# A GRU tile on TensorE: the sums' products ahead of the wait for the turned state, one PSUM bank moved from the ring of the sums to the candidate's state part

## The reference, cut to what matters

```python
h = relu(layernorm(x))
x = x + conv3(relu(conv2(relu(conv1(h)))))        # conv(h) = segment_sum((h @ W)[src] * norm, dst) + b
h = relu(layernorm(x))
red = segment_sum(h[src] + relvectors[rel], dst)  # 3125 x 256
gi, gh = red @ w_ih.T + b_ih, h @ w_hh.T + b_hh   # 3125 x 768 each
r = sigmoid(gi_r + gh_r);  z = sigmoid(gi_z + gh_z)
n = tanh(gi_n + r * gh_n)
x = x + (1 - z) * n + z * h
```

## Time and profile before

| what | value |
|---|---|
| runs | 934.06, 934.55, 934.75 us, median 934.55 |
| the profiled execution's own time | 933.93 us |
| its span, first to last instruction | 930.0 us |
| TensorE (PE) busy | 886.0 us, 95% |
| VectorE (DVE) busy | 444.3 us, 48% |
| ScalarE (ACT) busy | 290.0 us, 31% |
| granted TensorE clock, mean over the span | 0.992 |

### The profile page before, as it was taken

One profiled execution on the slowest core, in us unless ns is written; L12 is line 12 of the kernel. 1 busy time (PEld: TensorE's weight loads), 2 busy tenths in 40 slices (PEclk: granted clock), 3 DMA queues, 4 the chain that ended last, 5 costly groups with the idle time before them and its releaser, 6 DMA issues.

```text
span 930.0 us, 16580 instructions
## 1 busy us (share of the span) xinstructions
PE 886.0 (95%) x5495; PEld 529.4 (57%) x5495; DVE 444.3 (48%) x1164; ACT 290.0 (31%) x609; POOL 75.5 (8%) x244
## 2 busy tenths in 40 slices
PE   2779999999999999999999999999999999999996
PEld 1348777777777865444444544445464455555553
DVE  7956888888887201021112413336253133334345
ACT  3365566666666311011111202222231111222122
POOL 0210111000000025551000000000000000000000
PEclk9989999999999999999999999999999999999999
DMA  6100000000000410000000101111401000000101
GB/s 191 30 2 2 4 22 17 16 16 22 17 16 16 144 32 3 3 3 1 1 0 24 44 14 39 46 46 51 137 20 31 10 25 24 23 23 23 30 28 31
DMA packets 37009, 28.50 MB, mean 31 GB/s; under 512 B 12870, under 2 KB 35554, under 8 KB 36925
## 3 DMA queue, kind: packets, MB, share of 16 engines
q1 hardware_dynamic: 36252, 26.97, 9.6%
q10 hardware_dynamic: 672, 0.41, 0.2%
HBM read 17.56 MB, written 9.81 MB: 29 GB/s over the span
## 4 chain that ended last, share of the span: by engine, by line
PE 92%; DVE 5%; issue 1%; ACT 1%; SPq 0%; DMA 0%; DVEq 0%
PE ps L1233 42%; PE ps L905 12%; PE ps L807 10%; PE ps L642 9%; PE ps L1244 5%; PE ps L646 5%; PE ps L1263 2%; PE ps L886 2%; DVE node_b L914 1%; PE ps L842 1%; PE ps L854 1%; PE ps L874 1%; PE ps L627 1%; PE ps L818 0%; DMA count<-in_dst 0%
## 5 line engine op out<-in xcount | busy, mean ns | idle before, releaser
L1233 PE MATMUL ps<-count,node_b 128*128 128x512 f16 (+3 forms) x1400 | 270.5, 351 | 0.4 <-DVE node_b L1395 0.3
L807 PE MATMUL ps<-node_b 128*128 128x175 f16 x808 | 192.9, 259 | 13.7 <-issue 7.8
L1233 PEld LDWEIGHTS ps<-count,node_b 128*128 128x128 f16 (+2 forms) x1400 | 121.5, 98 | 142.1 <-issue 7.3
L905 PE MATMUL ps<-node_a,count 128*128 128x256 f16 x1050 | 200.7, 277 | 0.2 <-DVE node_a L1026 0.2
L914 DVE TENSOR_TENSOR node_b<-node_b 128x1024 f16<-128x1024 f16 (+2 forms) x303 | 161.7, 587 | 0.0
L1109 ACT ACTIVATE count<-ps 128x500 f32 x202 | 122.8, 608 | 96.7 <-PE ps L807 94.9
L1233 PE MATMUL ps<-count,node_a 128*128 128x512 f16 (+2 forms) x700 | 134.7, 352 | 0.0
L807 PEld LDWEIGHTS ps<-node_b 128*128 128x128 f16 x808 | 79.8, 99 | 62.7 <-issue 28.4
L905 PEld LDWEIGHTS ps<-node_a,count 128*128 128x128 f16 x1050 | 101.1, 100 | 4.2 <-ACT count L1109 0.4
L1233 PEld LDWEIGHTS ps<-count,node_a 128*128 128x128 f16 (+1 forms) x700 | 60.0, 97 | 73.9 <-issue 7.1
L1325 DVE SCALAR_TENSOR_TENSOR work<-ps,dinv,params 128x256 f32<-128x256 f32 (+1 forms) x25 | 12.0, 480 | 125.0 <-PE ps L1244 125.0
(11 more groups left out here) (210 smaller groups left out, 787.9 us busy)
## 6 DMA issues: line engine op xcount, KB each, us to landing
node_a<-in_x SPq DMA_DIRECT2D x4, 768.0 KB, 8.4
table_scratch<-agg SPq DMA_DIRECT2D x21, 128.0 KB, 1.8
node_b<-table_scratch SPq DMA_DIRECT2D x3, 768.0 KB, 6.6
xt<-x_scratch SPq DMA_DIRECT2D x16, 128.0 KB, 2.1
out<-scaled SPq DMA_DIRECT2D x16, 128.0 KB, 1.7
xt<-in_x SPq DMA_DIRECT2D x12, 128.0 KB, 2.0
params<-in_x SPq DMA_DIRECT2D x12, 128.0 KB, 2.0
x_scratch<-xt SPq DMA_DIRECT2D x12, 128.0 KB, 1.7
```

The lines of the kernel that those rows point to most:

```text
L807: return PE.matmul(window(s)[:, :, keys], low, key_hot[k][:, j, :, i].rearrange("p (t w) -> p t w", w=SPAN), start=(s == 0 and j == 0), st ...
L905: last = PE.matmul(out_slot(u)[0:m, :], count[:, t, u * P:u * P + m], node_a[:, t, part, :], start=(t == 0 and part == 0), stop=(t == T - ...
L1233: last = PE.matmul(ps[:, b, 0:cols], nodes[0:k, t, part, f * P:(f + 1) * P], count[0:k, t, c * CHUNK:c * CHUNK + cols], start=(n == 0 and ...
```

## The change

`AGG_RING` becomes 2, so that the groups of sums use banks 0 and 1 and TensorE waits ahead of group h for the evacuation of group h - 2, in all three stages. Bank 2 takes the candidate's state part. On TensorE, a GRU tile's two r and z matmuls from the sums are issued ahead of the wait for `h_out`; then come the two from the state, the candidate's two from the state (bank 2, behind a new wait `nh_read` for VectorE's read of the tile before, signal `nh_done`), and last the candidate's two from the sums (`n_done`). On VectorE, the state part is read after `nh_done`, the bias of the input part is added ahead of the wait for `n_done`, and the sum with PSUM comes last and releases the tanh. The matmuls, activations, VectorE operations and DMAs are the same in number and size.

```diff
--- before.py
+++ after.py
@@ -30,7 +30,7 @@
 SETTLE_FIRST, SETTLE_ODD, SETTLE_STEP = 11, 8, 17
 OUT_SLOTS = 3
 BEATS = 4
-AGG_RING = 3
+AGG_RING = 2
 LOADS = 4
 
 
@@ -232,7 +232,7 @@
         x1_tile = [xt[0][:, :], xt[1][:, :], piece(flat_a, D, F32)]
         h_tile = [scaled[0][:, :], scaled[1][:, :], piece(flat_a, D, F32)]
         AHEAD = len(x1_tile)
-        H_BANK, RZ_BANK, N_BANK = 3, (4, 5), (6, 7)
+        NH_BANK, H_BANK, RZ_BANK, NI_BANK = 2, 3, (4, 5), (6, 7)
         assert at_piece[0] <= T * 2 * D
 
 
@@ -559,8 +559,8 @@
         x1_in = [sem(f"x1_in{k}") for k in range(AHEAD)]
         out_done = [sem(f"out_done{k}") for k in range(AHEAD)]
         gru_w_in, gru_b_in = sem("gru_w_in"), sem("gru_b_in")
-        h_made, h_turned, h_out, rz_done, n_done, biased, gates, n_sum, n_due, new_n, z_used, result = (sem(n) for n in (
-            "h_made", "h_turned", "h_out", "rz_done", "n_done", "biased", "gates", "n_sum", "n_due", "new_n", "z_used", "result"))
+        h_made, h_turned, h_out, rz_done, nh_done, nh_read, n_done, biased, gates, n_sum, new_n, z_used, result = (sem(n) for n in (
+            "h_made", "h_turned", "h_out", "rz_done", "nh_done", "nh_read", "n_done", "biased", "gates", "n_sum", "new_n", "z_used", "result"))
 
         def gru_load_sp(order, i):
             t = order[i]
@@ -615,7 +615,7 @@
                 gru_turn_act(order, i + 1)
             ACTE.wait_ge(biased, i + 1)
             ACTE.activation(gate_rz[k][0:m, :], gate_rz[k][0:m, :], ACT.Sigmoid).then_inc(gates, 1)
-            ACTE.wait_ge(n_due, i + 1)
+            ACTE.wait_ge(n_sum, i + 1)
             ACTE.activation(work[k][0:m, :], work[k][0:m, :], ACT.Tanh).then_inc(new_n, 1)
 
         def gru_turn_pe(order, i):
@@ -632,25 +632,30 @@
             if i == 0:
                 gru_turn_pe(order, 0)
                 PE.wait_ge(gru_w_in, 32)
-            PE.wait_ge(h_out, i + 1)
             if i >= 2:
                 PE.wait_ge(n_sum, i - 1)
-            rz, nn = RZ_BANK[k], N_BANK[k]
+            rz, ni = RZ_BANK[k], NI_BANK[k]
             hs = [h_t[k][:, f, 0:m] for f in range(HALVES)]
-            for n, (l, w, f) in enumerate([(sums[f], w_ih_sb, f) for f in range(HALVES)] +
-                                          [(hs[f], w_hh_sb, f) for f in range(HALVES)]):
-                done = PE.matmul(ps[0:m, rz, 0:2 * D], l, w[:, f, 0:2 * D], start=(n == 0), stop=(n == 2 * HALVES - 1))
+            for f in range(HALVES):
+                PE.matmul(ps[0:m, rz, 0:2 * D], sums[f], w_ih_sb[:, f, 0:2 * D], start=(f == 0), stop=False)
+            PE.wait_ge(h_out, i + 1)
+            for f in range(HALVES):
+                done = PE.matmul(ps[0:m, rz, 0:2 * D], hs[f], w_hh_sb[:, f, 0:2 * D], start=False, stop=(f == HALVES - 1))
             done.then_inc(rz_done, 1)
-            for col, ls, w in ((0, sums, w_ih_sb), (D, hs, w_hh_sb)):
-                for f in range(HALVES):
-                    done = PE.matmul(ps[0:m, nn, col:col + D], ls[f], w[:, f, 2 * D:G], start=(f == 0), stop=(f == HALVES - 1))
+            if i:
+                PE.wait_ge(nh_read, i)
+            for f in range(HALVES):
+                done = PE.matmul(ps[0:m, NH_BANK, 0:D], hs[f], w_hh_sb[:, f, 2 * D:G], start=(f == 0), stop=(f == HALVES - 1))
+            done.then_inc(nh_done, 1)
+            for f in range(HALVES):
+                done = PE.matmul(ps[0:m, ni, 0:D], sums[f], w_ih_sb[:, f, 2 * D:G], start=(f == 0), stop=(f == HALVES - 1))
             done.then_inc(n_done, 1)
             if i + 1 < T:
                 gru_turn_pe(order, i + 1)
 
         def gru_tile_dve(order, i):
             m, k, slot = rows(order[i]), i % 2, i % AHEAD
-            rz, nn = RZ_BANK[k], N_BANK[k]
+            rz, ni = RZ_BANK[k], NI_BANK[k]
             rz_gate, v, h = gate_rz[k], work[k][0:m, :], h_tile[slot][0:m, :]
             if i == 0:
                 DVE.wait_ge(gru_b_in, 64)
@@ -660,15 +665,16 @@
             if i >= 2:
                 DVE.wait_ge(result, i - 1)
             DVE.tensor_tensor(rz_gate[0:m, :], ps[0:m, rz, :], bias_rz[0:m, :], ALU.add).then_inc(biased, 1)
-            DVE.wait_ge(n_done, i + 1)
-            DVE.tensor_tensor(v, ps[0:m, nn, D:2 * D], bias_hn[0:m, :], ALU.add).then_inc(*dve_seq.up())
-            DVE.wait_ge(*dve_seq.now)
+            DVE.wait_ge(nh_done, i + 1)
+            DVE.tensor_tensor(v, ps[0:m, NH_BANK, 0:D], bias_hn[0:m, :], ALU.add).then_inc(nh_read, 1)
+            DVE.wait_ge(nh_read, i + 1)
             DVE.wait_ge(gates, i + 1)
             DVE.tensor_tensor(v, v, rz_gate[0:m, 0:D], ALU.mult).then_inc(*dve_seq.up())
             DVE.wait_ge(*dve_seq.now)
-            DVE.tensor_tensor(v, ps[0:m, nn, 0:D], v, ALU.add).then_inc(n_sum, 1)
-            DVE.wait_ge(n_sum, i + 1)
-            DVE.tensor_tensor(v, v, bias_in[0:m, :], ALU.add).then_inc(n_due, 1)
+            DVE.tensor_tensor(v, v, bias_in[0:m, :], ALU.add).then_inc(*dve_seq.up())
+            DVE.wait_ge(*dve_seq.now)
+            DVE.wait_ge(n_done, i + 1)
+            DVE.tensor_tensor(v, ps[0:m, ni, 0:D], v, ALU.add).then_inc(n_sum, 1)
             DVE.wait_ge(new_n, i + 1)
             DVE.tensor_tensor(h, h, v, ALU.subtract).then_inc(*dve_seq.up())
             DVE.wait_ge(*dve_seq.now)
```

## The result

The changed kernel takes 943.94 us (median of four, 943.35 to 944.42) against 934.65 us before in the same session: a ratio of 1.010 with a 95% interval of 1.0082 to 1.0117. The forecast was 943.4. The profiled execution took 944.42 us with a span of 940.3, 10.3 us over the span before. In a bracketed wait, the name after the arrow is what ended it.)

The account below looks back on a forecast made before the run. TensorE, busy 95% of the span, was taken as the bound: 933.93 + 8.9 + 1.4 + 1.7 - 3.1 = 942.8 us, and with 0.6 us for the median 943.4, range 940.8 to about 945.7.

Parts of the forecast that it names:

- What bounds the kernel: Whole kernel: TensorE, busy for 95% of the span, bounds it; its waits leave almost nothing to absorb a new delay.
- The absorbed case: Rival: the stall is there, but TensorE's later waits shrink by as much, ending at 934 to 935 us; chance 0.02.
- Part 3, the ring: Groups of sums: with two banks TensorE waits for a short group's evacuation, 8.9 us in layer 2, 1.4 in layer 1.
- The faster rival: Rival: two banks are enough in layer 2, giving 932.8 us, or 931.4 if layer 1 is free too; chance 0.03.
- The three margins of 0.2 us: Second groups of other chunks: the evacuation fits by 0.2 us at three places, so zero cost, 0.2 each if misread.
- Part 4, the clock: After layer 2's stall: TensorE's granted clock falls to half, losing 1.7 us, bounds zero and 3.4.
- The trace has one case: Opening of the earlier trace: one low clock stretch of 3.4 us after 2.64 us idle, taken as the only one.
- the layer 1 stall: Layer 1, group of sums: a wait of 1.4 us for an evacuation, with its clock loss counted at nothing.
- Part 1: GRU tiles: sums' r and z matmuls cover the wait for the turned state, gaining 2.0 us plus 0.7 us.
- a tail wait: Last GRU tiles: each uncovered turn costs 0.22 us in place of 0.90, gaining 0.68, at three waits.
- The tiles with short sums: Three GRU tiles with halves of a 53-column group between, 0.77 us of matmuls hiding the wait: gain counted as nothing.
- Part 2: Last GRU tile: candidate's state part read early from its own bank, gaining 0.44 us, bounds 0.3 and 0.5; other tiles zero.

Follow-up runs that it names:

- Experiment 3: The changed kernel, ring of two, with ScalarE evacuating a chunk's first group ahead of the norm of the chunk before in layer 2: 931.88 us, ratio 0.9976.
- experiment 2: The kernel before with AGG_RING = 2 and nothing else: 947.31 us, ratio 1.0136.
- experiment 4: The changed kernel with 40 unread matmuls ahead of the wait in layer 2, keeping TensorE busy through the stall: 941.39 us, ratio 1.0073.
- experiments 5 and 6: 5: kernel before, only sums' r and z matmuls ahead of the wait, 930.63 us. 6: changed kernel, layers' ring three, all matmuls behind the wait, 933.91 us.

## Why the prediction was right, point by point

- **What bounds the kernel.** TensorE's waits had little reserve, and none absorbed the stall: everything after layer 2 came later by the whole of it. The reserve was read too small: the earlier trace rows are the two largest waits, and the same view has three more, of 0.7, 0.6 and 0.3 us, so 5.3 us in all and not 4. The absorbed case would have needed 9 and is out.
- **Part 3, the ring.** This carried the forecast, and its steps held to 0.1 us: the group to wait for, the evacuation's place behind the norm, the norm unmoved, 8.9 and 1.4 us. The order of ScalarE's queue was read from the code and its times from the earlier trace rows. Experiment 3 shows that it is order, experiment 2 that the constant alone does it. The faster rival went by durations; what that leaves out is that the evacuation has to be reachable in its engine's queue. It takes under 0.5 us for both short groups, but began at 531.35, 8.4 us after TensorE had made them (521.38 + 1.53). The Trainium skill, page "Perfetto Trace Analysis", section "Optimizing Tensor Performance", wants groups to rotate through banks so that one's evacuation overlaps the next one's matmuls; with two banks the groups rotate, and in this trace the overlap fails at the short ones.
- **The three margins of 0.2 us** held: the changed kernel has no wait of TensorE for line 1410 but the four shown. This was read, not tested by narrowing them.
- **Part 4, the clock.** Right in kind, mis-sized: 1.7 us forecast, 2.9 in the trace, 2.6 in the times of experiment 4. The term was half of a low stretch of 3.4 us, read at one place. Here the clock was low for 10.2 us, and the group ran through 5.8 of them (531.69 to about 537.5), half of which is the 2.9. The size lay inside the bounds of 0 and 3.4.

"The trace has one case" was a misreading. The trace of the kernel before has three more low stretches, from 60.9, 67.7 and 98.5 us, again of 3.4 us each, and the last follows a wait of only 1.41 us:

```profile
96.82 0.26 PE L807 MATMUL ps<-node_b 128*128 128x175 f16 x1 [1.41 <-DVE node_b L914]
...
98.00:102.00 4.00, 4.00 (x28) 3.20 (x28) 3.63 (x10) 1.35 (x3) 1.45 (x1) 0.57 0.00 0
```

Nor does the length carry over from one execution to the next. Behind the same pause of 2.64 us the changed kernel's trace is low for 6.8 us (from 42.6), already when TensorE restarts at 43.10, and then for 10.2 us from 63.1:

```profile
43.10 1.07 PE L813 MATMUL ps<-node_b 128*128 128x175 f16 x3 [2.64 <-issue]
...
43.00:49.00 6.00, 5.83 (x18) 1.98 (x19) 6.00 (x14) 1.36 (x4) 0.88 (x1) 0.50 0.00 0
```

So the length was not to be had from one stretch of one execution, and what decides it stays open; the runs show what it cost here. That the layer 1 stall cost nothing at the clock held (11.07 us for the group behind it), but with a wait of 1.41 us followed by a fall elsewhere in the trace it was not as safe as it was put.
- **Part 1** gave 3.3 us where 2.7 were forecast. The gain for a tail wait was 0.76 us and not 0.68, since the first four records of a tile are quicker too (1.72 us from the first to the fifth and not 1.79), the bound that I had given at 0.75; the first tile gained 0.80 for the same reason. The tiles with short sums gained 0.19 together where I counted none. Before, they began 0.90 to 0.95 us after the turn, like those of the tail, so the wait set it; now they begin 0.83 to 0.88 us after it, behind the short matmuls.
- **Part 2** had the right size, but the gain is not its own alone. Either part by itself earns the 0.44 us (experiments 5 and 6); the sum came out right because it counted them once.
- **The total.** The measured parts sum to 1.5 us more than the forecast ones: 1.2 are the clock, 0.8 the opening phase that differs between executions and 0.1 the stall in layer 1, less 0.6 of larger gains. Against the median the forecast was only 0.5 us low. That closeness is in part luck: the clock's error of 1.2 us and the gains' of 0.6 have opposite signs. The opening phase hardly enters there, since the medians (943.94 - 934.65 = 9.3 us) are of several executions, and the 0.6 us that the forecast added for the median over the profiled execution stand for most of it.

## What to carry to other kernels

A ring's depth is to be checked against the order of the engine that empties it, at the shortest item above all: here groups of 11 us passed with two banks, by an estimated 0.2 us at three places, and one group of 1.4 us stalled TensorE for 8.8 us behind work that it had nothing to do with. Before a buffer is given up, test whether the reorder that it pays for still gains once the other edits are in; here the gain was already taken. And where TensorE is made to pause, price the restart too, from every low stretch of the clock in the trace and not from the first one found.

## What the runs showed of the hardware

The restart cost was larger than I had expected, and hardly hung on the pause between 4.45 and 8.77 us: after 8.77 us idle the next group of 50 matmuls lost 2.9 us, after 4.45 us idle 2.5 us, while after 1.30 us idle in layer 1 it took 11.07 us, as at a full clock. Filling the whole pause with unread matmuls is worth 2.6 us, although these matmuls do nothing for the result.
